# Products of ones in nine pauses of TensorE, in a four-layer kernel on one core

## The reference

```
x = adapter(x, domain)          # down 256->64, gelu, expert matrix of the domain, up 64->256, residual, layernorm
x = attention_block(x, t, ...)  # layernorm * (1+scale(t)) + shift(t); 16 heads of 16 with additive bias and mask;
                                # output projection; layernorm; 256->1024, gelu, 1024->256
x = rotate(x, theta, phi)       # pairs of features turned by two angles of each sequence
x = x_plus_moe(x, subject)      # layernorm, style norm over tokens, router, top 2 of 8 experts,
                                # each 256->1024, relu, 1024->256, weighted sum, residual
```

## Time and profile before

| | |
|---|---|
| median of three runs | 674.24 us |
| lowest, highest | 673.66, 674.68 us |
| the profiled execution's own time | 675.41 us |
| its span, first to last instruction | 673.5 us |
| mean granted TensorE clock | 0.906 |
| TensorE matmul busy | 553.9 us (82%) |
| VectorE busy | 459.7 us (68%) |
| ScalarE busy | 308.2 us (46%) |
| GpSimd busy | 222.5 us (33%) |
| shares of the chain that ended last | PE 49%, DVE 25%, ACT 7%, DMA 7%, issue 6% |

### The profile page before, as it was taken

The page is one execution under the profiler, slowest core; times in us unless marked ns, Lnnn a source line. Parts: engine busy times, 40 slices in busy tenths (PEclk is TensorE's granted clock), DMA queues, the critical chain, the costliest instruction groups (busy, mean ns, idle before and its releaser), DMA issues.

```text
span 673.5 us, 15380 instructions
## 1 busy us (share of the span) xinstructions
PE 553.9 (82%) x4840; PEld 411.5 (61%) x4841; DVE 459.7 (68%) x1284; ACT 308.2 (46%) x643; POOL 222.5 (33%) x137
## 2 busy tenths in 40 slices
PE   2479479899588996789767599899799999999992
PEld 0437365486564765646666258686676778777771
DVE  5666994899969799664896926886544556464651
ACT  2329356535473355643533233657554434443440
POOL 2240614048226254161540602022631322131322
PEclk9568598999797998979979599999999999999997
DMA  6985019431376331665307657763532213122220
GB/s 196 307 226 182 4 48 235 163 96 64 125 134 212 126 126 52 156 201 187 126 36 242 239 220 291 266 215 67 165 55 43 42 36 49 34 42 38 50 36 0
DMA packets 41176, 86.36 MB, mean 128 GB/s; under 512 B 7321, under 2 KB 31938, under 8 KB 37026
## 3 DMA queue, kind: packets, MB, share of 16 engines
q1 hardware_dynamic: 21248, 56.47, 24.4%
q0 software_dynamic: 8352, 16.99, 13.7%
q10 hardware_dynamic: 11522, 12.20, 6.3%
HBM read 57.10 MB, written 29.44 MB: 128 GB/s over the span
## 4 chain that ended last, share of the span: by engine, by line
PE 49%; DVE 25%; ACT 7%; DMA 7%; issue 6%; ACTq 3%; POOL 2%; SPq 1%; DVEq 0%; POOLq 0%
PE bank L1931 9%; PE bank L1746 6%; PE bank L1920 5%; PE bank L1922 5%; PE bank L1921 4%; PE bank L1932 4%; DMA stage<-in_moe_w 3%; DVE sc_sum L1137 2%; PE bank L1726 2%; PE bank L1755 2%; DVE stats L1057 2%; PE bank L1710 2%; ACTq L880 2%; PE bank L1700 2%; ACT split L684 2%
## 5 line engine op out<-in xcount | busy, mean ns | idle before, releaser
L1920 PE MATMUL bank<-xs_f,w_moe 128*128 128x128 f16 x624 | 123.1, 221 | 12.0 <-ACT stage L892 6.4
L892 ACT ACTIVATE stage<-bank,cols 128x128 f32<-128x128 f32 x312 | 88.4, 375 | 78.4 <-PE bank L1922 40.3
L1922 PE MATMUL bank<-xs_f,w_moe 128*128 128x128 f16 x624 | 123.1, 221 | 0.0
L1921 PE MATMUL bank<-xs_f,w_moe 128*128 128x128 f16 x624 | 122.6, 220 | 0.0
L645 POOL DMA_INDIRECT out_x<-x_kept,ids x39 | 63.5, 1628 | 167.6 <-DVE x_kept L1518 102.9
L1920 PEld LDWEIGHTS bank<-xs_f,w_moe 128*128 x624 | 61.1, 98 | 48.4 <-issue 20.2
L1931 PE MATMUL bank<-w_moe,split 128*128 x208 | 79.2, 383 | 0.5
L1024 DVE SCALAR_TENSOR_TENSOR split<-stage,split 128x2048 f16<-128x2048 f32 x16 | 41.0, 2563 | 37.8 <-ACT split L684 37.8
L1746 PE MATMUL bank<-w_moe 128*128 128x512 f32 x128 | 61.1, 639 | 5.0 <-ACT w_moe L754 5.0
L1921 PEld LDWEIGHTS bank<-xs_f,w_moe 128*128 x624 | 61.4, 98 | 2.8
L557 POOL TENSOR_TENSOR w_moe<-w_moe,sc_max 128x2048 f32<-128x2048 f32 x8 | 29.0, 3620 | 100.6 <-DVE sc_max L1132 100.6
(11 more groups left out here) (272 smaller groups left out, 1172.4 us busy)
## 6 DMA issues: line engine op xcount, KB each, us to landing
stage<-in_moe_w SPq DMA_DIRECT2D x16, 1024.0 KB, 7.6
w_split<-split SPq DMA_DIRECT2D x16, 1024.0 KB, 5.0
w_moe<-w_split SPq DMA_DIRECT2D x8, 2048.0 KB, 8.7
w_moe<-in_bias POOLq DMA_DIRECT2D x8, 1024.0 KB, 9.6
xs<-dispatched ACTq DMA_DIRECT2D x41, 130.0 KB
w_moe<-in_x_f SPq DMA_DIRECT2D x4, 512.0 KB, 7.8
w_moe<-in_x_t SPq DMA_DIRECT2D x4, 512.0 KB, 12.7
out_x<-x4b ACTq DMA_DIRECT2D x4, 512.0 KB, 3.0
```

Of the source, the lines that this page charges most:

```text
L892: ins = act.activation(h32[j][:, f, :], bank[banks + g][:, P * (f % 4):P * (f % 4) + P], ACT.Relu, bias=moe_b1[:, bass.ds(e, 1), f], scale ...
L1920: pe.matmul(o, hi, xs_f[j][:, k, :], start=(k == 0), stop=False)
L1921: pe.matmul(o, hi, xs_f[j][:, KD + k, :], start=False, stop=False)
L1922: mm = pe.matmul(o, lo, xs_f[j][:, k, :], start=False, stop=(k == KD - 1))
```

## The change

A helper `keep_clock(free_bank, count)` is added to TensorE's program. It issues `count` products of the f16 tile `ones` (128x128, loaded each time) with itself, its columns repeated four times to 512, into a PSUM bank that nobody uses at that time. Nothing reads the results, and the products have no waits of their own. It is called in seven places of the source, which are executed as nine groups with 168 products in all:

| group | place | products |
|---|---|---|
| G1 | before `turn1(0)` | 34 |
| G2 | after `up_projection(1)`, before `context(0, 0)` | 32 |
| G3 | after `turn1(1)`, before `queries(1)` | 9 |
| G4 | c = 1, 2: before `context(c + 1, 0)`, behind the waits for q_ready and k_ready | 7, 15 |
| G5 | c = 0, 1, 2: before `turn3(c)` | 20, 15, 18 |
| G6 | before `turn2(3)` | 18 |

```diff
+            def keep_clock(free_bank, count):
+
+                for _ in range(count):
+                    pe.matmul(bank[free_bank][:], ones[:], ones[:].unsqueeze(1).broadcast_to([P, 4, P]),
+                              start=True, stop=True)
+
...
             mm.then_inc(setup_pe, 1)
+            keep_clock(4, 34)
             turn1(0)
...
             up_projection(1)
+            keep_clock(5, 32)
             context(0, 0)
             context(0, 1)
...
             output_projection(0)
             turn1(1)
+            keep_clock(5, 9)
             queries(1)
...
                     pe.wait_ge(k_ready.sem, k_ready.of(c + 2, 1))
+                if c > 0:
+                    keep_clock(4, (7, 15)[c - 1])
                 context(c + 1, 0)
+                keep_clock(4, (20, 15, 18)[c])
                 turn3(c)
...
             c = NCH - 1
+            keep_clock(1, 18)
             turn2(c)
```

## The result

The changed kernel takes 666.43 us (median of 6 runs, 665.41 to 669.37); the kernel before, run beside it and before, 673.95 (6 runs). The ratio is 0.9905 with a 95% interval of 0.988 to 0.993: 6.4 us faster, with 4.7 to 8.1 as bounds.

A forecast was written before the change was run, and what follows sets the result against it. TensorE, slowed to half clock behind its pauses, held about half the chain; long pauses ended on other engines. Gains of 1.8 + 0.5 + 0.3 + 0.4 + 1.6 = 4.6 us from median 674.24 gave 669.6, range 664.5 to 675.5.

The forecast's parts named there:

- G3: Products before queries(1): the half-clock stretch from 102.76 goes, queries and keys take 7.03 for 8.83 us; -1.8, bounds 0 and -1.8.
- G6: Products before turn2(3): turn starts 0.2 to 1.7 us later, feed-forward takes 14.0 for 15.92; -1.6, between -1.2 and -1.9.
- The signs named ahead: Expected in the profile: queries(1) about 7.1 us, turn3(0) about 1.05, pass 3's first feed-forward 14.0, mean clock near 0.94.
- The price of ones: One 512-column product of ones on TensorE: 0.22 us at full clock with its weight load hidden, 0.43 at half clock.
- Does the clock follow ones?: Assumed yes: products of ones lift TensorE's clock as real data do, after 3.13 to 6.07 us of dense work.
- rival (3): Slower: groups starting at half clock do not lift the clock in time; 684 us, chance 0.13 including a milder form.
- G1 and G2: Before turn1(0) and context(0, 0): worth 0 each, from -0.2 to +0.4 and from -0.1 to +0.5 us.
- G5, c = 0: Products before turn3(0): turn3(0) and context(1, 1) at full clock, ScalarE setting the pace; -0.5 us, no more than -1.8.
- G4 and G5, c = 1: Around context(2, 0), before turn3(1): -1.3 us gain, possible overrun 1.3 to 2.8; -0.3, between -1.3 and +1.5.
- G4 and G5, c = 2: Around context(3, 0), before turn3(2): context at full clock, 3.3 us stay empty and the clock falls; -0.4, between 0 and -1.5.
- Rival (1): More than forecast: untouched half-clock stretches at 205.16 to 211.98 and 297.32 to 300.73 move away; 4.6 to 9.7 us, chance 0.17.

The follow-up runs named there:

- the repetition: The changed kernel run once more with no edit, on a chip where both are slower: 673.87 against 679.48 us for the kernel before, ratio 0.9911.

## Why the prediction was right, point by point

- **Direction and size.** Forecast -4.6, just outside the interval of the measured -6.4 (4.7 to 8.1); the time, 666.43, is inside the stated range. The mechanism holds: eight columns in place of 512 took the whole gain away. The signs named ahead came too: queries(1) in 7.13, turn3(0) in 1.09, the last feed-forward in 14.00, a mean clock of 0.943. How near the size came is partly luck: 1.8 of the 4.6 is G3's, worth about 0 alone, and the terms that hold make 2.8.
- **The price of ones.** 0.22 and 0.43 were right: 4.49 us for 20, 3.14 for 7 at 0.50, weight loads hidden. The 131 ns of the Trainium skill (TensorE: Matmul & The Clock Gate, section Back-to-back issue gap) appear in no group.
- **Does the clock follow ones?** Yes, after 3.95 and 4.13 us, inside the 3.13 to 6.07 of the earlier trace rows. In the other traces that have G1, its 34 products took 8.9 to 10.3 us, so it rose there too. With it rival (3), 684 us, is out. The reading by how busy the engine is was the right one.
- **G1 and G2: 0.** The lead is 1.61 at `up_projection(0)` and 1.63 at `queries(1)`, so 66 of the 168 products bring nothing in the rows. In time, 0 to 2 us stay open (without them 0.9931, with them 0.9905 and 0.9911).
- **G3: 1.8 forecast, 1.7 in the rows, about 0 in value when alone.** This is the step that was wrong in kind. It took the stretch at 102.76 as something that an empty pause of 2.61 us brings and G3 removes. But two traces with that pause empty (2.61 and 2.40 us) had no fall behind it, and with G3 the stretch came behind the next pause, before the feed-forward, in 6 of 7 traces. In the first profile after it did not come (14.00), which is why that trace shows the full 1.7.
- **G5, c = 0: 0.5 forecast, 1.0 measured** (7.93 became 6.93). ScalarE was less in the way than I had it: its copies at L744 began 2.0 us behind the turn, where I had 2.4, and the products of L1716 began 3.75 behind it, where my sum has 4.2. The repetition also shows 1.0.
- **G4 and G5, c = 1: -0.3 forecast.** Both halves came, larger: the stretch from `turn3(1)` on took 6.9 instead of 8.7 (-1.8, forecast -1.3), and the overrun was 2.0 (forecast 1.3 to 2.8 if the clock falls ahead of k_ready, and it did, at 246.79). Net +0.2 in that trace, and the same in the repetition. Leaving the seven out ended the overrun; nine ahead of the waits did so too, and in the rows no more.
- **G4 and G5, c = 2: -0.4 forecast, -1.1 measured** in the profile. The 3.3 us stayed empty as forecast (3.28) and the clock fell, but for 3.41 us and not 6.07. In the repetition the pause was the same (3.28) and the gain 0.0: 9.92 us from `turn3(2)` to `output_projection(3)`, 9.91 before.
- **G6: -1.6 forecast, -1.9 in the rows** of the changed kernel, -1.4 with G6 alone. The turn was 0.2 and 1.2 late (forecast 0.2 to 1.7), ScalarE's slack took most of it, and the feed-forward ran 14.00 both times. In the repetition it is -1.6, as forecast.
- **Rival (1)**, given 0.17, is what the first profile shows on top: neither 205 to 212 nor 297 to 301 was at 0.50, worth 3.3 and 1.7 where they stand. Of the 3.3, 2.3 went in the longer pause at k_ready. And luck has a part: in the next five traces that hold G4 and G5 and leave their pauses empty, the feed-forward of pass 1 is at 15.7 again in two and that of pass 2 in three, while the latter took 14.00 in three kernels with nothing filled near it (eight columns, G3 alone, G6 alone). This is the reason why that profile leads by more than the ratio.
- **Sum.** The terms without G3 make 2.8 forecast; measured in rows 1.0 - 0.2 + 1.1 + 1.9 = 3.8 in the first profile and 1.0 - 0.2 + 0 + 1.6 = 2.4 in the repetition, with G3 1.7 and 0. In the first profile what the two stretches of rival (1) leave, 2.2, makes it the 7.7 of the passes. Of the 6.4 by the ratio, 2.6 to 4.0 are thus assigned to no group for certain, against 2.4 to 3.8 that are: the falls that come or stay away in the feed-forwards differ by 1.7 us each between executions, and one profile for each kernel does not average them.

## What to carry to other kernels

A pause filled with idle products is worth the slower work behind it only if the next empty pause isn't met by dearer work: list all pauses, not the longest, and judge a filling by the sum from one common step to the next. Before you put a slow stretch down to the pause in front of it, look at a second execution: here the same pause was followed by a fall in one and not in another. Products behind the semaphore wait of a pause delay the work, at half clock the more: seven of them took 3.1 us and made a turn 2.0 us late. Ahead of the wait, or left out, they did not. Count a filling by chain: 66 products in places where the chain ran over other engines brought nothing in the rows. And a fall behind which another wait stands can cost nothing: 1.7 us more in a feed-forward of pass 1 only made the next pause shorter.

## What the runs showed of the hardware

- Products of ones in f16, into a bank that nobody reads, raised the granted clock from 1.2 to 2.4 GHz after 3.95 and 4.13 us, as real data did; products with 8 columns in the same number (34 in 1.07 us) did not, and the turn behind them took 1.97 us. They kept TensorE busy for 1.07 us only, so this does not show that narrow products as such don't count.
- Short pauses count: 1.89 us empty in front of the feed-forward were followed by a fall in one execution of the changed kernel (15.70 us) and not in another (14.00). 2.61 us empty in front of queries(1) were followed by one in the kernel before (8.83) and not with G4 and G5 alone (7.13).
- The recorded clock can be wrong in the opening: in the kernel with G3 alone it reads 1.00 throughout 15 to 38 us, but the turn at 34.17 took 1.97 us, the time at half clock. Mean clocks of such executions (0.927 there) are too high; the time of a known piece of work is the check.
- Two executions of the same start differed by 1.6 us before any of the changed code. The kernel before had medians of 673.95, 677.62, 679.48 and 674.34 us in the four sets of runs, up to 5.5 us apart, so each kernel was compared only with the kernel before on the same chip.
